# Attention in one decoder layer: stacks loaded during the projection, side products placed by time, shift and copies moved off VectorE, filler products on TensorE

## The reference

```python
def _L0_attn_ref(x, ...):
    q = _apply_rope(proj(WQ_w, WQ_b)); k = _apply_rope(proj(WK_w, WK_b)); v = proj(WV_w, WV_b)
    scores = einsum('bhqd,bhkd->bhqk', q, k) / sqrt(16)
    attn = softmax(where(causal, scores, -inf)); out = einsum('bhqk,bhkd->bhqd', attn, v)
...
def _L0_xattn_ref(q, kv, Wq, Wkv, Wc):
    idx = argmax(einsum('bld,bmd->blm', qp, kv)); mem = kv[idx]      # mk, mv from mem @ Wkv
    attn = softmax(einsum('bhld,bmd->bhlm', qh, mk) * scale)
...
x = _layernorm(x + _L0_attn_ref(x, ...))
x = _layernorm(x + _L0_xattn_ref(x, ctx_1024, ...))
return _layernorm(x + _L0_ffn_ref(x, ...))
```

## Time and profile before

| | us |
|---|---|
| median of three runs (lowest, highest) | 1347.91 (1340.49, 1356.87) |
| the profiled execution, its own time | 1346.86 |
| span of the profiled execution | 1345.1 |
| PE busy | 1171.4 (87%) |
| DVE busy | 951.2 (71%) |
| ACT busy | 604.0 (45%) |
| POOL busy | 125.1 (9%) |

### The profile page before, as it was taken

One profiled execution on the slowest core, in us unless ns is written; L12 is line 12 of the kernel. 1 busy time (PEld: TensorE's weight loads), 2 busy tenths in 40 slices (PEclk: granted clock), 3 DMA queues, 4 the chain that ended last, 5 costly groups with the idle time before them and its releaser, 6 DMA issues. The chain is left out here.

```text
span 1345.1 us, 17831 instructions
## 1 busy us (share of the span) xinstructions
PE 1171.4 (87%) x6638; PEld 695.9 (52%) x6638; DVE 951.2 (71%) x2160; ACT 604.0 (45%) x805; POOL 125.1 (9%) x132
## 2 busy tenths in 40 slices
PE   7729999999999999873999469999976799999997
PEld 3414444343443333243788333333335589999997
DVE  4638777878878997237589369999927475757575
ACT  1201334646746766841333005566663434544442
POOL 2400000010010000143000000500004000000000
PEclk9955557969969999986999559999998889999999
DMA  7431166900000000041210394200012000000000
GB/s 266 178 87 35 28 69 76 113 7 2 2 1 1 1 1 2 1 132 33 87 53 1 42 102 50 96 2 2 3 33 72 1 1 1 17 1 17 1 17 16
DMA packets 34020, 55.55 MB, mean 41 GB/s; under 512 B 6162, under 2 KB 16840, under 8 KB 33352
## 3 DMA queue, kind: packets, MB, share of 16 engines
q1 hardware_dynamic: 33928, 54.34, 19.3%
HBM read 38.47 MB, written 14.89 MB: 40 GB/s over the span
## 5 line engine op out<-in xcount | busy, mean ns | idle before, releaser
L543 ACT ACTIVATE self_probs<-self_scores 128x1024 f32<-128x1024 f32 (+3 forms) x320 | 272.0, 894 | 244.9 <-PE self_scores L496 243.8
L481 PE MATMUL self_max<-stack_k,stack_q 48*128 48x512 f32 (+3 forms) x640 | 254.5, 504 | 43.6 <-DMA stack_k<-ones 24.0
L572 DVE TENSOR_REDUCE self_piece_max<-self_max 128x1 f32<-128x512 f32 x384 | 244.9, 685 | 50.3 <-PE self_max L481 49.2
L481 PEld LDWEIGHTS self_max<-stack_k,stack_q 48*128 48x128 f32 x640 | 126.3, 222 | 226.0 <-DVE self_piece_max L572 127.7
L496 PE MATMUL self_scores<-stack_q,stack_k 50*128 50x512 f32 (+3 forms) x640 | 190.1, 450 | 7.2 <-DMA stack_q<-self_shift 4.5
L572 DVE TENSOR_REDUCE cross_piece_max<-cross_max 128x1 f32<-128x512 f32 x256 | 159.5, 684 | 27.1 <-PE cross_max L481 26.7
L543 ACT ACTIVATE cross_probs<-cross_scores 128x1024 f32<-128x1024 f32 x128 | 124.3, 1022 | 109.6 <-PE cross_scores L496 109.5
L509 PE MATMUL self_out<-self_probs,V 128*17 128x512 f32 (+3 forms) x1280 | 168.9, 604 | 2.3 <-ACT self_probs L543 1.7
L568 DVE CUSTOM_DVE_ANT_0 self_junk<-self_max,causal_sb 128x128 bf16<-128x128 f32 (+3 forms) x256 | 115.8, 486 | 25.2 <-PE self_max L481 24.5
L481 PE MATMUL cross_max<-kx_few,stackx 49*128 49x512 f32 x256 | 104.1, 504 | 27.0 <-DMA stackx<-ones 17.3
L1242 ACT ACTIVATE o_tok<-ph 128x512 f32<-128x512 f32 x96 | 57.4, 598 | 143.7 <-PE ph L93 137.5
(11 more groups left out here) (196 smaller groups left out, 1711.6 us busy)
## 6 DMA issues: line engine op xcount, KB each, us to landing
stack_q<-qparts SPq DMA_DIRECT2D x96, 64.0 KB, 2.8
stackx<-xparts SPq DMA_DIRECT2D x24, 256.0 KB, 10.2
stack_k<-kparts SPq DMA_DIRECT2D x18, 256.0 KB
qparts<-parts SPq DMA_DIRECT2D x8, 512.0 KB, 2.8
kparts<-parts SPq DMA_DIRECT2D x8, 512.0 KB, 2.8
cross_raw<-in_w SPq DMA_DIRECT2D x4, 768.0 KB, 4.8
n_raw<-in_w SPq DMA_DIRECT2D x6, 512.0 KB, 4.2
xT_sb<-in_xT SPq DMA_DIRECT2D x4, 512.0 KB, 8.3
```

The lines of the kernel that those rows point to most:

```text
L481: mm = nc.tensor.matmul(slot[:, 0:pc["w"]], pc["lhsT"], pc["rhs"], start=True, stop=True)
L543: nc.scalar.activation(probs[:, i % 3, 2 * pair:2 * pair + 2, st["off"]:C], ps[:, 2 * pair:2 * pair + 2, st["off"]:C], ACT.Exp, scale=SCAL ...
L572: ins = nc.vector.tensor_reduce(to, slot[:, 0:pc["w"]], AX.X, ALU.max)
```

## The change

It has five parts.

1. **Early stacks.** The mask, the ones and the loads of group 0 for the chunks 0, 1 and 2 are issued by SP inside the projection's block: after unit 5, 9 and 13 of `units`, once the parts of the chunk before have landed, 12 DMAs each. Only chunk 3 is left to the attention block's start, and the loads of the later groups follow the shifts of the units, two chunks per unit. `MKV_AT` goes from 3 to 2, and the split and write of `mk_parts` stand between the last units instead of behind them.
2. **Side products by time.** `EVEN` is gone. `schedule` gives each product and each step a length in ns and deals products in proportion to the step's length, so narrow steps get fewer and full ones more.
3. **Shift off VectorE.** At a turn ACT copies minus the transposed maxima into `lowered`, POOL makes the two parts, and the slot is free when ACT is done. The memset is gone.
4. **The copy of a unit's output** (`acc`) is made by ACT.
5. **Products that nobody reads** on PE: 12 of 512 columns at the end of the projection, one of 256 columns behind each product ahead of step 0, and 12 more behind the turn of unit 0, in both attentions.

In the cross-attention the loads of the expert weights are also issued one per unit, and POOL splits each behind a shift (before: all behind one another).

```diff
-EVEN = 4
+FILL = 12
+LEAD_NS = 5000.0
...
-                MKV_AT = 3
+                MKV_AT = 2
...
                             sp.dma_start(dst, parts[:, n % 4].bitcast(F32)).then_inc(s_parts_out[n % 4], 16)
...
+                            if c and n % 4 == 1:
+                                for i in range(4):
+                                    sp.wait_ge(s_parts_out[i], 16 * c)
+                                load_stack(sp, c - 1)
+                            if n == MK_UNIT + 2:
+                                sp.wait_ge(mk_rest, 1)
...
+                        for _ in range(FILL):
+                            nc.tensor.matmul(pk[:, 1], w_sb[:, 2, 0, 0:P], xT_sb[:, 0, 0:C], start=True, stop=True)
...
+                    def cost(item):
+
+                        if item[0] == "piece":
+                            return works[item[1]]["pieces"][item[2]]["w"] / 0.96 + 75.0
+                        return 100.0 if item[0] == "turn" else 700.0
+
+                    spans = [4 * (C - st["off"]) / 1.4 + 350.0 for st in steps]
...
+                        done = ends[at - 1]
+                        due = done + rate * spans[i]
+                        for u in range(len(works)):
+                            end = ends[where[("turn", u)]]
+                            room = begins[first_of[u]] - begins[i] - LEAD_NS
+                            if first_of[u] > i and end > done:
+                                due = max(due, done + (end - done) * spans[i] / room if room > spans[i] else end)
                         need = at
...
-                        need = min(max(need, min(at + EVEN, len(order))), len(order))
+                        while need < len(order) and ends[need] <= due:
+                            need += 1
...
+                                pool.wait_ge(turned, u + 1)
+                                if u >= 2:
+                                    pool.wait_ge(shift_in[u % 2], 64 * (u // 2))
+                                nc.gpsimd.tensor_copy(shift[:, u % 2, 0], lowered[:, u % 2]).then_inc(shift_high, 1)
+                                pool.wait_ge(shift_high, u + 1)
+                                nc.gpsimd.tensor_tensor(shift[:, u % 2, 1], lowered[:, u % 2], shift[:, u % 2, 0].bitcast(F32),
+                                                        ALU.subtract).then_inc(shift_ready, 1)
...
                             for item in before:
                                 side_item(item)
+                                nc.tensor.matmul(ps[:, 0, 0:D], ident[:], ones[:], start=True, stop=True)
+                            for _ in range(FILL):
+                                nc.tensor.matmul(ps[:, 0, 0:D], ident[:], ones[:], start=True, stop=True)
...
+                                    nc.scalar.activation(lowered[:, u % 2], slot[0:UR, 0:P], ACT.Copy, scale=-1.0).then_inc(turned, 1)
...
+                                    act.wait_ge(probs_used, i)
+                                    nc.scalar.copy(acc_sb[:, u % 2], po[:]).then_inc(acc_copied, 1)
...
-                                    nc.vector.tensor_scalar(shift[:, u % 2, 0], slot[0:UR, 0:P], -1.0, None, ALU.mult).then_inc(shift_high, 1)
-                                    dve.wait_ge(shift_high, u + 1)
-                                    nc.vector.scalar_tensor_tensor(out=shift[:, u % 2, 1], in0=slot[0:UR, 0:P], scalar=-1.0,
-                                                                   in1=shift[:, u % 2, 0], op0=ALU.mult,
-                                                                   op1=ALU.subtract).then_inc(shift_ready, 1)
...
-                                    nc.vector.memset(mark[:], 0.0).then_inc(side_read, 1)
...
-                                    nc.vector.tensor_copy(acc_sb[:, u % 2], po[:]).then_inc(acc_copied, 1)
```

244 lines of the change are left out of this document (148 added, 96 removed).

## The result

The changed kernel took 1372.34 us (median of four runs, 1369.61 to 1373.61) beside 1345.55 for the kernel before (four runs, 1340.49 to 1356.87): a ratio of 1.0185, with a 95% interval from 1.0116 to 1.0253. It is slower by 27 us, where 30 us faster was forecast and 1341 was the upper end of the range.

What follows compares the result with a forecast made beforehand. PE was taken to set the pace at half clock, DVE at full clock and in the cross-attention. Terms -2 - 6 - 5 - 17 = -30 gave a span of 1315 and a time of 1317 us, range 1284 to 1341.

Steps and rivals of the forecast that it cites:

- Front of the self-attention: Stretch up to the first scores: no 24 us wait for loads, against queue, filler and hop costs; -2, bounds -2.5 and +11.
- Part (b): Fillers ahead of the self-attention's step 0: 16 pairs with products take 11 us at full clock, 19 at half.
- dear end: Self-attention front all at half clock: pairs take 19 us, twelve fillers 11.3, first scores at 109.
- rival A: Fillers bring the full clock into the self-attention's first stretch, 98.42 to 200.47: 16 us more go, time 1289; chance 0.15.
- Part (a): SP's queue at the projection's end: twelve load issues of 5.8 us ahead of the last writes, partly covered by POOL; 3 taken.
- Part (c): Behind the self-attention's first turn: fillers cover the shift's wait of 4.55 us, to which the ACT-to-POOL hop adds some 0.5.
- Cross-attention's front: Fillers ahead of step 0: +2 to +3 at full clock, +19 if all ran at half; +3 taken.
- both fronts being cold at once: Both attentions' fronts at half clock: +13 and +16 on the forecast, chance 0.04.
- Steps and spells of the self-attention: Steps -6 from relieved DVE and reordered products; half-clock spells -5, half of 11.2 us, from the copy on ACT.
- Steps of the cross-attention: DVE loses copy and turn, -17.9, all showing; ACT's order +2; two steps fewer without products -4.
- C: Rival: narrow groups leave PE waiting and the clock falls at each unit end; 1367, decided from seven spells on; chance 0.07.
- B: Rival: the self-attention yields nothing, +14 on the forecast and perhaps another 5; 1330 to 1340; chance 0.2.

Runs made afterwards that it cites:

- e6: The changed kernel without any fillers, the twelve loads of chunk 2 issued at the self-attention block's start: 1324.40 us, ratio 0.9806 to the kernel before.
- e1: The changed kernel with all three groups of fillers removed: 1332.47 us, ratio 0.9885 to the kernel before.
- e8: The kernel before with one part alone, the copy of each unit's output on ACT: 1346.75 us, ratio 0.9963.
- e5: The changed kernel without fillers and with the old dealing of side products (at least four per step): 1338.58 us, ratio 0.9933 to the kernel before.
- e11: As e6, plus 16 fillers back to back at the start of the cross-attention's block: 1326.63 us, ratio 0.985 to the kernel before.
- e12: As e6, with the turn on DVE and a unit's output transposes one step later: 1307.43 us, ratio 0.9704 to the kernel before.

## Why the prediction was wrong

- **Front of the self-attention, forecast -2, measured +18.5.** Part (b), the fillers, failed, first in its price: 16 pairs of product and filler took 27.4 us, above the 19 that were the dear end. And it failed in its choice: "with fillers it is busy nearly throughout, as it is in the stretches of full clock, so I stay near the lower end". PE was busy throughout and the clock stayed at half. The same prediction held, in its rival A, the row that spoke against this choice, where PE was busy 97.51 of 102.05 us at 0.50, and used it only on the later stretch. The dear end gave 109; 116.09 came, of which 3.9 us are the later start. Without fillers the front is -3.3. Part (a), the queue, was right in its mechanism and half its size: 3 us of 5.8 taken, 6.1 measured (e6), since POOL's end covers half of the issues, as reckoned, but three writes stand behind the loads and take longer to land. Part (c), the hop, was right (0.57 for 0.5).
- **Cross-attention's front, forecast +3, measured +20.8.** The same step; its bound of +19 was near it and was written off as both fronts being cold at once, "+13 and +16", a chance of 0.04. The two are not independent chances, they are one mechanism.
- **Steps and spells of the self-attention, forecast -6 and -5, measured -6.0 together, -11.8 without the fillers (e1).** That e1 meets the sum of -11 is in part luck, since its terms moved: the narrow groups gained 1.9 us each and not 1.2, full steps lost more, and both spells of the earlier trace rows ended, where half of them was counted and all of that given to the copy; the order had the larger part. The copy's 0.60 us in units at full clock was right (e8). Of the 5.8 us between e1 and the changed kernel 4.8 lie in unit 3, part of which ran at half clock there.
- **Steps of the cross-attention, forecast -20, measured -7.2.** "Since DVE sets the step" (the prediction's reason why all of it shows) failed. DVE was busy 174.05 of 185.67 us there, but PE was busy 174.48 of them in the same row, and the prediction set PE's share aside because single steps showed ACT waiting for PE behind waits for slots. A relief that was priced at 1.23 us a unit took a unit of the old order from 11.79 to 11.46 us (before to e5). Together with the new order the steps got 7.2 us shorter: units 0 to 3, relieved of 15 products, take 57.5 us against 67.1, units 4 to 13, with 11 more, 119.3 against 118.6, and the last two, with 4 more, 19.1 against 17.1.
- **The rivals.** C had the sign but not the place: behind unit 3 the changed kernel has one spell of half clock, of 3 us (457 to 461), where C needed seven. B's place, the self-attention, yielded what was forecast; its +14 adds up to only +11 from the terms that it names (+26 for +22, and no -7). A was right to doubt itself: the fillers did not carry the full clock through step 0 of the self-attention. What was missing is the rival "fillers at half clock cost their time in both fronts, and nothing follows", a mechanism to which its own dear bounds gave 13 + 16 = 29 us on the forecast, 1346; 38 came.

Without fillers the change is faster than the kernel before by 1.2% (e1), and with the loads of chunk 2 late by 1.9% (e6).

## What to carry to other kernels

When work is put on an engine "where it would idle", ask what that engine is asked for next. Here PE's idle time ahead of step 0 was the pace of DVE, and each filler stood in front of the product that DVE waited for.

Before crediting a relief of the bounding engine in full, add up the next engine's own work over the same unit. With DVE and PE both near 95%, 1.23 us of relief brought 0.33 here (old order), though the copy alone brought 0.56 of 0.60 in the new one. Test it by halving one engine's work.

When an edit is costed at nothing or half because other work covers it, look at when the cover ends, at what else stands behind the edit in the same queue, and at whether the same change moves the cover. And before two orders are compared unit by unit, count what a unit holds in each.

## What the runs showed of the hardware

- The clock stays at half with PE busy 27.44 of 27.45 us by the profile, in products of 48 rows alternating with full fillers, and opens in the midst of fillers that follow one another (at 112.5 us in the changed kernel, at 754 in e11). So a busy share near 1 in the profile is not a sign of the full clock.
- An opened clock did not last: it was at half again 3 us into step 0 of the self-attention, where PE was busy 1.87 of 3.40 us, and 5 us into the steps of the cross-attention, where PE was busy 4.25 of 5.30 us. In e11 it fell in the 5.6 us in which PE waited for the loads.
- The same fp32 filler of 256 columns takes 1.15 us at half clock between products with other weights, and 0.85 us behind another filler.
- DVE's sum or difference of two SBUF tiles (128x512, into `whole`) took 1.85 and 2.97 us while POOL worked in SBUF, and 0.68 to 0.69 us in the fourteen cases in which it did not (e6).
- The clock's course differs between executions of nearly the same program: behind the half-clock stretches at the self-attention's start it stays full from 167 to 525 us in e12, from 252 to 457 in the changed kernel, and from 221 to 323 in e6. Units 1 and 2 together take 76 to 91 us. Differences under 10 us between medians of four runs of such kernels have to be read from units at equal clock, not from the total.
